# Two diffusion-transformer layers on one core: hyperbolic half-steps spread over seven positions, side jobs moved out of the score pairs

## The reference, cut to what matters

```python
# layer 0: 16 heads, queries are the normed input itself, values are 32 wide per head
scores = einsum(Q, K) + causal_mask;  o = softmax(scores) @ V;  x + gelu(o) @ Wf + bf
# layer 1: 16 heads of 8: six plain, four hyperbolic, six with normalised q and k
outs = [sdpa(q[:6], k[:6], v[:6]), hyp_attn(q[6:10], k[6:10], v[6:10], curv), sdpa(qn, kn, v[10:])]
# hyp_attn: arg = max(-curv * inner, 1 + 1e-7); dis = sqrt(1/curv) * arccosh(arg)
#           scores = 1 / (eps + dis) + causal_mask; softmax(scores) @ v
```

## The kernel before, in words

| stage | engine, line | lag |
|---|---|---|
| scores | PE L762 | 0 |
| arg and its square form | DVE L1367, L1372 | 1 |
| root (Ln, Exp) | ACT L1033, L1034 | 1 |
| sum | POOL L1693 | 1 |
| log | ACT L1039 | 2 |
| linear | POOL L1689 | 2 |
| score (Ln, Exp) | ACT L1044, L1045 | 3 |
| shift by the maximum | DVE L1380 | 3 |
| exponential, causal cut | ACT L1050, POOL L1611 | 4 |
| values ("hv"), for two half-steps at once | PE L706, DVE L1333 | 5 |

## Time and profile before

### The profile page before, as it was taken

The page is one execution under the profiler, slowest core; times in us unless marked ns, Lnnn a source line. Parts: engine busy times, 40 slices in busy tenths (PEclk is TensorE's granted clock), DMA queues, the critical chain, the costliest instruction groups (busy, mean ns, idle before and its releaser), DMA issues. The chain is left out here.

```text
span 2831.1 us, 30019 instructions
## 1 busy us (share of the span) xinstructions
PE 2278.3 (80%) x10649; PEld 853.8 (30%) x10649; DVE 1483.1 (52%) x3046; ACT 1358.9 (48%) x1924; POOL 802.8 (28%) x918
## 2 busy tenths in 40 slices
PE   6898668887788598887778859878877885987789
PEld 2333322222224343222222434322222243422134
DVE  6553445655545544565554544566555354367742
ACT  1445335456564333545566332454555633258932
POOL 1111102223331233222233124222323212435624
PEclk7999755966789698686778869879577786975789
DMA  5001321011003242001101224201000123301022
GB/s 144 19 2 46 88 47 33 18 33 25 18 11 98 70 130 74 18 18 33 25 18 31 90 58 137 67 18 33 17 18 18 31 90 90 98 31 33 7 62 90
DMA packets 79350, 140.39 MB, mean 50 GB/s; under 512 B 11636, under 2 KB 32244, under 8 KB 74580
## 3 DMA queue, kind: packets, MB, share of 16 engines
q1 hardware_dynamic: 79200, 138.46, 17.5%
HBM read 122.04 MB, written 15.20 MB: 48 GB/s over the span
## 5 line engine op out<-in xcount | busy, mean ns | idle before, releaser
L1303 DVE TENSOR_REDUCE mx<-ps 128x1 f32<-128x512 f32 (+3 forms) x992 | 612.0, 655 | 312.0 <-PE ps L678 249.7
L1060 ACT ACTIVATE pr<-ps 128x1024 f32<-128x1024 f32 (+3 forms) x672 | 515.1, 803 | 361.4 <-PE ps L748 360.9
L748 PE MATMUL ps<-qop,kop 75*128 75x512 bf16 (+7 forms) x1344 | 461.7, 407 | 139.1 <-ACT pr L1060 87.2
L675 PE MATMUL ps<-kop,qop 72*128 72x512 bf16 (+7 forms) x1248 | 453.0, 395 | 100.8 <-DVE mx L1303 78.7
L789 PE MATMUL ps<-pr,vt 128*32 128x512 f32 (+3 forms) x2688 | 393.8, 668 | 32.6 <-POOL pr L1603 22.0
L1603 POOL TENSOR_SCALAR_AFFINE_SELECT pr<-pr 128x512 f32<-128x512 f32 x224 | 151.8, 678 | 603.7 <-ACT pr L1060 601.4
L1112 ACT ACTIVATE pr<-ps 128x512 f32<-128x512 f32 x224 | 133.7, 597 | 312.1 <-PE ps L873 245.4
L675 PEld LDWEIGHTS ps<-kop,qop 72*128 72x128 bf16 (+1 forms) x1248 | 131.1, 107 | 479.9 <-DVE mx L1303 312.1
L748 PEld LDWEIGHTS ps<-qop,kop 75*128 75x128 bf16 (+1 forms) x1344 | 127.7, 111 | 422.7 <-ACT pr L1060 188.7
L883 PE MATMUL ps<-pr,turn_w 128*128 128x512 f32 x384 | 194.8, 594 | 4.5 <-POOL pr L1594 4.1
L678 PE MATMUL ps<-maskqk,identb 128*128 128x128 bf16 x832 | 196.0, 257 | 0.0
(11 more groups left out here) (313 smaller groups left out, 3081.8 us busy)
## 6 DMA issues: line engine op xcount, KB each, us to landing
wb<-gates_scratch SPq DMA_DIRECT2D x192, 256.0 KB, 3.3
kop<-kparts_scratch SPq DMA_DIRECT2D x32, 576.0 KB
qop<-qparts_scratch SPq DMA_DIRECT2D x96, 192.0 KB
nbc<-hmax_scratch SPq DMA_DIRECT2D x8, 1024.0 KB, 5.6
xin<-in_x SPq DMA_DIRECT2D x7, 512.0 KB, 5.7
kparts_scratch<-on SPq DMA_DIRECT2D x12, 256.0 KB, 3.5
qparts_scratch<-on SPq DMA_DIRECT2D x12, 256.0 KB, 4.1
qparts_scratch<-wb SPq DMA_DIRECT2D x12, 192.0 KB
```

What stands on the lines that cost most here:

```text
L675: mm = pe.matmul(o, qop[0:k, slot(b, n), j, qb * P:(qb + 1) * P], kop[0:k, slot(b, n), j, k0:k0 + wd], start=True, stop=not diag)
L748: mm = pe.matmul(o, kop[0:k, slot(b, n), 2 * pair + j, kb * P:(kb + 1) * P], qop[0:k, slot(b, n), 2 * pair + j, q0:q0 + wd], start=True, s ...
L1060: nc.scalar.activation(pr[:, g % 3, 2 * pair:2 * pair + 2, o0:o0 + wd], ps[:, bank:bank + 2, o0:o0 + wd], ACT.Exp).then_inc(J.exps, 1)
L1303: ins_ = nc.vector.tensor_reduce(mx[:, ring(b, n), j0:j0 + heads, qb, col % 2], ps[:, bank, 0:heads * wd].rearrange("p (j n) -> p j n", j= ...
```

## The change

1. The lags become named constants. Root goes from 1 to 2, sum with it, log from 2 to 3, linear with it, score from 3 to 4, shift from 3 to 5, exponential and cut from 4 to 6, values from 5 to 7. Arg stays at 1.
2. In the middle blocks the half-steps 8 to 23 stand three positions earlier (29 instead of 32, and so on); the last position stays 85.
3. PE's side jobs: inside a pair one stands now only in block 0. Behind each pair one stands as before. In blocks 1 to 4 `values` takes one between its value matmuls and its sums, in units of layer 0 only.
4. In the middle blocks the pieces of an ordinary unit are spread over one position more, so "maxima" and "max" stand one position later.
5. In block 4 the ring of buffers has ten places instead of eight.

```diff
--- before.py
+++ after.py
@@ -115,9 +115,11 @@
 def hyp_positions(b):
 
     if 1 <= b < B:
-        return [3 + 3 * k if k < 8 else 32 + 3 * (k - 8) for k in range(HYP_HALVES)]
+        return [3 + 3 * k if k < 8 else 29 + 3 * (k - 8) for k in range(HYP_HALVES)]
     return [2 + k for k in range(HYP_HALVES)] if b == B else []
 
+
+ARG_LAG, ROOT_LAG, LOG_LAG, SCORE_LAG, SHIFT_LAG, EXP_LAG, HV_LAG = 1, 2, 3, 4, 5, 6, 7
 
 HYP_POS = [hyp_positions(b) for b in range(B + 2)]
 
@@ -150,7 +152,7 @@
 
 
 def positions(b):
-    return max([std_steps(b)] + [p + 6 for p in HYP_POS[b][-1:]]) + (b > 0)
+    return max([std_steps(b)] + [p + HV_LAG + 1 for p in HYP_POS[b][-1:]]) + (b > 0)
 
 
 def score_jobs(b):
@@ -211,19 +213,19 @@
         for c in range(NC):
             plan[c].append(("out", (c,)))
     for i in range(NS if HYP_POS[b] else 0):
-        plan[HYP_POS[b][2 * i + 1] + 5].append(("hv", (i,)))
+        plan[HYP_POS[b][2 * i + 1] + HV_LAG].append(("hv", (i,)))
     if b == 0:
         unit_pieces(0, -1, -1)
         for n in range(1, 4):
             unit_pieces(n, NS * (n - 1), NS * n - 4)
     elif b < B:
         hyp_pieces(0, 0, 1)
-        unit_pieces(1, 2, 8)
-        unit_pieces(2, 15, 20)
+        unit_pieces(1, 2, 9)
+        unit_pieces(2, 15, 21)
         hyp_pieces(1, 24, 28)
-        unit_pieces(3, 28, 32)
+        unit_pieces(3, 28, 33)
         for n in (4, 5, 6):
-            unit_pieces(n, NS * (n - 1) + 3, NS * (n - 1) + 8)
+            unit_pieces(n, NS * (n - 1) + 3, NS * (n - 1) + 9)
         for c in range(NC):
             plan[36 + c].append(("xT", (c,)))
     else:
@@ -235,7 +237,7 @@
         if layer(b, n):
             plan[min(p + 2, end)].append(("turn", (i, n, c)))
     for c in range(NC if HYP_POS[b] else 0):
-        plan[HYP_POS[b][2 * (4 + 8 * c) - 1] + 6].append(("turn", (NOBODY, HYP, c)))
+        plan[HYP_POS[b][2 * (4 + 8 * c) - 1] + HV_LAG + 1].append(("turn", (NOBODY, HYP, c)))
     n = 0
     for p in sorted(plan):
         items = []
@@ -438,7 +440,7 @@
             z = [hB.rearrange("p (j n) -> p j n", j=2), tmp.rearrange("p (j n) -> p j n", j=2),
                  wb[:, 1, 0:2], wb[:, 1, 2:4]]
             if b == B:
-                z += [on[:, i, :].rearrange("p (j n) -> p j n", j=2) for i in range(4)]
+                z += [x.rearrange("p (j n) -> p j n", j=2) for x in [on[:, i, :] for i in range(4)] + [hA, xT(b)]]
             z = z[k % len(z)]
             return z[:, :, q0 - c * CH:q0 - c * CH + wd]
 
@@ -747,7 +749,7 @@
                             o = ps[:, bank + j, o0:o0 + wd]
                             mm = pe.matmul(o, kop[0:k, slot(b, n), 2 * pair + j, kb * P:(kb + 1) * P],
                                            qop[0:k, slot(b, n), 2 * pair + j, q0:q0 + wd], start=True, stop=True)
-                            if j == 0 and extra and (pair or layer(b, n) == 0):
+                            if j == 0 and extra and b == 0:
                                 side_job(*extra.pop(0))
                         mm.then_inc(J.scores, 1)
                         if extra:
@@ -765,7 +767,7 @@
                                        start=True, stop=True)
                     mm.then_inc(h_prod, 1)
 
-                def values(g):
+                def values(g, extra):
                     n, s = divmod(g, NS)
                     l, u = UN[b][n]
                     c, kb, q0, wd, diag = STEPS[s]
@@ -790,6 +792,8 @@
                                        pr[:, g % 3, j, o0:o0 + wd], start=kb == 0, stop=last,
                                        tile_position=(0, 32 * j))
                     if l == 0:
+                        if extra and b:
+                            side_job(*extra.pop(0))
                         for j in range(4):
                             mm = pe.matmul(ps[32 * j:32 * j + 32, 5, o0:o0 + wd], ones32[:],
                                            pr[:, g % 3, j, o0:o0 + wd], start=kb == 0, stop=last,
@@ -808,7 +812,7 @@
                     if p + 1 < steps:
                         scores(p + 1, extra)
                     if p < steps:
-                        values(p)
+                        values(p, extra)
                     for x in extra:
                         side_job(*x)
                     if hyp_at(b, p) != NOBODY:
@@ -1072,7 +1076,8 @@
                 for p in range(positions(b) + 1):
                     if p < steps:
                         std_exp(p)
-                    for lag, stage in ((4, hyp_exp), (3, hyp_score), (2, hyp_log), (1, hyp_root)):
+                    for lag, stage in ((EXP_LAG, hyp_exp), (SCORE_LAG, hyp_score), (LOG_LAG, hyp_log),
+                                       (ROOT_LAG, hyp_root)):
                         if hyp_at(b, p - lag) != NOBODY:
                             stage(hyp_at(b, p - lag))
                     n, s = divmod(p, NS)
@@ -1385,9 +1390,9 @@
                     for i in range(len(OUTS[b])):
                         if OUTS[b][i][0] == p:
                             outputs_out(i)
-                    shift = hyp_at(b, p - 3)
-                    if hyp_at(b, p - 1) != NOBODY:
-                        hyp_arg(hyp_at(b, p - 1))
+                    shift = hyp_at(b, p - SHIFT_LAG)
+                    if hyp_at(b, p - ARG_LAG) != NOBODY:
+                        hyp_arg(hyp_at(b, p - ARG_LAG))
                     first = len(SIDE[b][p]) // 2 if shift != NOBODY else 99
                     for x in SIDE[b][p][:first]:
                         side_job(*x)
@@ -1678,16 +1683,16 @@
             for p in range(positions(b) + 1):
                 if p < steps:
                     cut(p)
-                if hyp_at(b, p - 4) != NOBODY:
-                    hyp_cut(hyp_at(b, p - 4))
-                k = hyp_at(b, p - 2)
+                if hyp_at(b, p - EXP_LAG) != NOBODY:
+                    hyp_cut(hyp_at(b, p - EXP_LAG))
+                k = hyp_at(b, p - LOG_LAG)
                 if k != NOBODY:
                     pool.wait_ge(h_log, k + 1)
                     for i in range(2):
                         j = 2 * (k % 2) + i
                         z = hyp_z(b, k)[:, i]
                         nc.gpsimd.tensor_scalar(z, z, hyp[:, 4 + j:5 + j], HYP_EPS, ALU.mult, ALU.add).then_inc(h_lin, 1)
-                k = hyp_at(b, p - 1)
+                k = hyp_at(b, p - ROOT_LAG)
                 if k != NOBODY:
                     pool.wait_ge(h_root, k + 1)
                     nc.gpsimd.tensor_tensor(hyp_z(b, k), hyp_z(b, k), hyp_x(k), ALU.add).then_inc(h_sum, 1)
```

## The result

The kernel with the change takes **2681.49 us** (median of 3 runs, 2676.12 to 2702.96) against 2820.79 before. The ratio is 0.9534, 95% interval 0.9444 to 0.9625, so it is faster by 139 us. Ratios here are taken from executions in the faster of the two states that the clock's records show, so they need not be the quotient of the medians beside them.

The account below looks back on a forecast made before the run. In the middle blocks no engine is full: fixed-order queues wait on each other and PE pays in idle time and clock. Terms: -20 per middle block, -60 for three, block 4 -8, together -68: 2820.8 to 2753 us; range 2680 to 2845.

Parts of the forecast that it names:

- Root, -23: Each middle block: with root one position later, PE's waits for ACT behind the root go, -23 us; bounds 0 and 41.5.
- pairs in one piece, -3: Each middle block: pairs ready one or two pieces earlier shorten PE's waits for ACT, -3 us; between 0 and 9.
- Job between values and sums, -6: Each middle block: DVE can reduce three pieces, not two, during values and sums; -6 us, between -6 and 18 gained.
- hv -2: Each middle block: hv falls between pairs where the second waits for arg; 2 of 10.1 us gained, between 0 and 7.
- Maxima one position later, +15: Middle-block unit ends: PE stands for DVE's copy and three DMAs, 2.5 us at six units, +15; between 0 and +29.
- Sum and shift, +5: Each middle block: POOL's sum delays DVE's shift 14 us, PE feels a third, +5 us; between 0 and +28.
- Clock, -6: Each middle block: the granted clock rises as PE's idle time falls by some 14 us, -6 us; between 0 and 35.
- the text's own sign: Sign of a wrong forecast: middle blocks under 410 us, which only the clock can do; about 430 us was expected.
- The rival of the clock: Middle blocks' granted clock rises to 0.82, each gains 30 us more, 2663 us in all; chance 0.13.
- the 29 of that rival: Middle-block units stand 4.8 us for maxima's rows at six places, 29 a block; root gives half; 2887 us; chance 0.13.
- POOL's hold on DVE: Middle blocks: 24 sums each delay the shift 2.35 us, PE pays 56 instead of 5; 2906 us; chance 0.07.
- Block 4, -8: Block 4, bound by ACT: longer lags and ten buffers let ACT run through, -8 us; between 0 and -16.

Follow-up runs that it names:

- e2_slots: Only the new places of PE's side jobs, put into the kernel before; 2816.01 us, ratio 0.9997 to the kernel before.
- e6: The whole change, but only root is one position later and log, score, shift, exp follow at old distances (lags 1, 2, 3, 4, 4, 5, 6); 2751.93 us, ratio 0.9779.
- e12: The whole change, but root, log and score keep old lags; only shift, exp and hv are two positions later; 2778.57 us, ratio 0.9891 to the kernel before.
- e3: Only the pieces spread over one position more, maxima one position later, put into the kernel before; 2795.9 us, ratio 0.9955.
- e1_lags: The change without new side-job places and spread: only longer lags, moved half-steps and ring of ten; 2695.88 us, ratio 0.9590 to the kernel before.
- e9_fill: The whole change plus six thrown-away 512-column matmuls before the wait for the maxima's rows at middle-block unit starts; 2689.39 us, ratio 0.9554 to the kernel before.
- e5_lags_pieces: The whole change with PE's side jobs back in their old places, so lags and spread only; 2708.04 us, ratio 0.9625 to the kernel before.

## Why the prediction was right in sign and too small in size

The direction and its main reason held: the gain is in the middle blocks, and it began with ACT no longer standing before the root. Term by term for block 2, predicted and measured:

- **Root, -23, and pairs in one piece, -3.** Both were to come out of PE's waits for ACT, and they can't be told apart there. The wait for the exponentials went from 26.8 to 4.0, for the cut from 5.7 to 2.3, for the reciprocal, which was counted as gone, from 3.2 to 3.7: -25.7 against -26. Right in sum. The pairs' share is not shown: with the new places alone (e2_slots) these waits did not fall. And e6 and e12 show that the root's wait is not all of it: with that wait gone and shift and exponential a position earlier 9.4 us remain, with these two late and the root early 15.1. The later stages were no side remark.
- **Job between values and sums, -6.** Meant to take from the maxima's 20.0; these went up to 26.1. Wrong in sign as a wait. That DVE's reductions are late next once PE comes faster is the likely reason; the lags alone, with the old places, have 22.7.
- **hv -2.** The wait for arg went from 10.1 to 6.7, -3.4. Right.
- **Maxima one position later, +15.** A new 16.9 for the rows and 3.8 more for the joined maxima, 20.7: inside the bounds of 0 and 29, with the floor of 3.2 us exactly as block 0 had it. In size it was about right; its source is only in part the later position, since 7.1 us of the wait for the rows are there with the lags alone. As a price it was wrong: e3 adds just the spread and is 0.45% faster, or the same.
- **Sum and shift, +5.** The case is real (3.42 us instead of 1.22), and removing the sum brings a middle block 1.5 to 5.3 us. Not contradicted, but within the scatter of a block.
- **DVE's stand for ACT's score**, 59.2 us in block 2, went to nothing. The text put the shift at nothing because it was on no path; what its stand cost PE was not measured by itself.
- **PE's wait for ACT before hyperbolic scores**, 5.8 in the earlier trace rows, fell to 0.8; no term had it.
- **Idle time in all:** 84.3 to 75.3, 9.0 less, where the terms made 14.
- **Clock, -6.** PE's busy time fell by 34.2 us in block 2 and by 110 in the three. This is the step that failed. The terms without the clock made 14 us a block and the trace gives 10; the clock term was 6 and the trace gives 37 on average, above even the 35 that I had as its bound.

The clock term was mis-sized because of what it was tied to. I read from three stages that idle share and clock go together, and let the clock rise only in so far as the idle share fell. In these runs that link doesn't hold. PE's idle time in the three middle blocks and their granted clock were 255 us and 0.74 before, 259 and 0.77 with e12_exp_only, 235 and 0.77 with e6_root_only, 192 and 0.79 with e1_lags, 178 and 0.79 with e9_fill, 226 and 0.81 with the change. The kernels with the least idle time have not the highest clock, and the one with as much as before has a higher one. What does part them is the lags: the three kernels with the old ones run at 0.74 to 0.75, all with new ones at 0.77 or more. (The half-steps moved by three positions go with the lags in every run, so they aren't parted from them.) The clock was at its lower level in 70 stretches before and 43 after, but this count doesn't follow the clock in the other runs either: 59 with e1_lags at 0.79, 45 with e5_lags_pieces at 0.77. Nor does the number of PE's stands of over 0.1 us, 356 before, 295 after and 269 with e5_lags_pieces. Why the clock is higher stays open: filling the stand for the rows doesn't raise it (e9_fill), the total of idle time isn't it, and how the idle time and PE's side jobs lie between the matmuls inside a unit was not tried by itself. The Trainium skill (TensorE: Matmul & The Clock Gate, "A second HAM failure mode: psum-queue depth-cycling") describes a kernel in which small idle times between groups of matmuls made the clock swing between its two levels. The clock does swing here, 70 times in three blocks before, but no run here isolates small idle times as the cause.

So the text's own sign came out: middle blocks under 410 were said to be what "only the clock can do", and they are at 402 to 407. The rival of the clock was the right mechanism: it had 36 us a block from the clock (the 6 and 30 more), and 37 were found. The low chance that I gave it rested on the same idle share. That the range held, by 1.5 us, is owed to the part of it that was kept for this rival; the forecast's own range, 2710 to 2790, did not hold. It took some luck as well: two other misses went against the clock's, 4 us less of idle time a block and 14.5 us in block 4, and without them the time would have been near 2655, below the range (an estimate from these stages). The rivals on the slow side fell: the wait for the rows and the joined maxima rose by 20.7 us, under the 29 of that rival, and the root gave all, not half; POOL's hold on DVE is worth a few us a block at most and not 56. In that rival's sum a third of the 51 us makes 2804 and not 2820.

**Block 4, -8.** It was +6.5. The step that failed is that ACT runs through once the root has room. ACT's wait for the root, 16.5 us, became one of its stage exponential for the shift, 18.0 us where it had been 3.6; half-steps are one position apart there, and the wait came back at a later link of the chain. The rest goes with PE's clock, as above. Of what was tried, only shortening the sum brought the block under the 200.0 us of before with the side jobs in their new places (194.5 us).

## What to carry to other kernels

Where PE runs at a mixed clock, price a removed wait twice: the idle time, and the clock, with the whole distance between the clock now and that of a stretch of the same instructions that runs well as its upper bound; don't scale the second by the idle share. When a stage's engines share a repeating pattern of positions, look at every engine for waits on a stage of the same position, and for a pile-up of work at one: here moving the root alone gave 2.2%, moving the stages behind it alone 1.1%, both 4.7%. And a wait that a trace lets you size exactly, as the one for the rows of maxima, can still cost nothing: with the spread alone PE's other waits fell by as much as this one rose.

## What the runs showed of the hardware

- The granted clock is not set by PE's idle share alone: 0.74 at 18.9% and 0.81 at 18.6%, with the same instructions.
- Filling a stand of 2.8 us at each unit's start with matmuls did not raise the clock right after it by more than 0.04 (0.55 and 0.57 without, 0.59 and 0.60 with it).
- The clock differs between executions of the same code by enough to matter: block 2 took 413.2 us at 0.78 and 406.7 at 0.81 in two kernels that differ only in block 4.
- A DVE add with two SBUF inputs that started 0.02 us after a POOL add of 2.36 us took 3.42 us instead of 1.22, so it moved only when POOL was done. Of the change's 48 shifts of 128x1024, the 31 that overlap a POOL operation take 1704 ns on average, the other 17 take 1216.
